# Attention with shared key projections: two batches a matmul, the last key apart, 64-row products in halves of the array

## What is computed

```python
q = (layernorm(x) @ Wq + bq)        # x: 64 x 32 x 256
k = (ctx @ Wk + bk)                 # ctx: 64 x 257 x 192, Wk: 192 x 256
v = (ctx @ Wv + bv)
attn = softmax(clip(q . k * 0.25, -1e4, 1e4))   # per batch, 16 heads of 16
x = x + (attn @ v) @ Wo + bo
```

## Time and profile before

| | before |
|---|---|
| median of 3 runs | 633.14 us (629.55 to 634.79) |
| the profiled execution | 629.26 us, its span 627.5 us |
| granted TensorE clock, mean of the profiled execution | 0.989 |
| busy: PE, PEld, DVE, ACT, POOL | 95%, 77%, 73%, 54%, 53% |
| first stage, start of the first projection to the last scores | 15.6 to 333.1 us |
| the rest up to the end of the span | 333.1 to 627.5 us |

### The profile page before, as it was taken

One profiled execution on the slowest core, in us unless ns is written; L12 is line 12 of the kernel. 1 busy time (PEld: TensorE's weight loads), 2 busy tenths in 40 slices (PEclk: granted clock), 3 DMA queues, 4 the chain that ended last, 5 costly groups with the idle time before them and its releaser, 6 DMA issues. The chain is left out here.

```text
span 627.5 us, 21706 instructions
## 1 busy us (share of the span) xinstructions
PE 596.4 (95%) x8364; PEld 484.3 (77%) x8364; DVE 459.9 (73%) x1073; ACT 339.7 (54%) x743; POOL 331.5 (53%) x482
## 2 busy tenths in 40 slices
PE   9999999999999999999999999896999999998786
PEld 3788878888788887888886788773578888884574
DVE  3687877888678786777776755989799977773453
ACT  3677868788688776778774346541222233330121
POOL 3357858777677885788872322221433333306561
PEclk9999999999999999999999999996999999999999
DMA  8624643766355836973300992119533433435774
GB/s 242 154 68 108 175 167 110 237 180 206 115 172 162 215 127 202 231 209 123 123 3 22 413 412 99 35 49 373 183 127 128 141 136 126 129 116 154 207 210 117
DMA packets 65204, 102.10 MB, mean 163 GB/s; under 512 B 15408, under 2 KB 42096, under 8 KB 64080
## 3 DMA queue, kind: packets, MB, share of 16 engines
q1 hardware_dynamic: 59808, 86.42, 42.7%
q0 software_dynamic: 4432, 13.50, 7.8%
q10 hardware_dynamic: 864, 0.79, 0.5%
HBM read 69.42 MB, written 31.26 MB: 160 GB/s over the span
## 5 line engine op out<-in xcount | busy, mean ns | idle before, releaser
L537 DVE TENSOR_SCALAR Pm<-scores 128x514 f32<-128x514 f32 x128 | 88.1, 688 | 57.0 <-PE scores L750 56.9
L653 ACT ACTIVATE Pm<-Pm,nm 128x257 f32<-128x257 f32 x256 | 115.8, 505 | 2.5 <-DVE nm L542 2.5
L542 DVE TENSOR_REDUCE nm<-Pm 128x2 f32<-128x514 f32 x128 | 87.5, 684 | 2.2
L1634 POOL DMA_INDIRECT Xg<-y_d,inv x39 | 37.1, 951 | 87.1 <-PE scores L1821 69.9
L648 ACT ACTIVATE PT<-bank 128x512 f32<-128x512 f32 x64 | 38.2, 598 | 74.5 <-PE bank L761 74.5
L731 PE MATMUL bank<-hA,wH 128*128 128x258 f32 x256 | 75.3, 305 | 0.1
L738 PE MATMUL bank<-wH,hA 128*128 128x256 f32 x256 | 74.3, 301 | 0.5 <-DVE PT L549 0.5
L761 PE MATMUL bank<-cst,Pm 128*128 128x128 f32 x512 | 69.9, 279 | 0.0
L731 PE MATMUL bank<-hA,wL 128*128 128x258 f32 x256 | 69.1, 280 | 0.0
L738 PE MATMUL bank<-wL,hA 128*128 128x256 f32 x256 | 68.9, 280 | 0.0
L1836 PE MATMUL bank<-W,xh 128*128 x208 | 66.7, 402 | 1.0 <-DVE xl L1744 1.0
(11 more groups left out here) (262 smaller groups left out, 1442.2 us busy)
## 6 DMA issues: line engine op xcount, KB each, us to landing
w_d<-whl SPq DMA_DIRECT2D x64, 256.0 KB, 3.4
W<-w_d SPq DMA_DIRECT2D x8, 2048.0 KB, 15.4
g_d<-gg SPq DMA_DIRECT2D x39, 256.0 KB
wst<-in_W1T SPq DMA_DIRECT2D x32, 256.0 KB, 3.6
cx<-in_ctxT SPq DMA_DIRECT2D x31, 258.0 KB, 2.9
cx<-in_ctxT SPq DMA_DIRECT2D x62, 129.0 KB, 3.5
bb<-in_b SPq DMA_DIRECT2D x8, 512.0 KB, 12.6
xb<-in_x SPq DMA_DIRECT2D x4, 512.0 KB, 5.5
```

What stands on the lines that cost most here:

```text
L537: v.tensor_scalar(Pm[:, i % 2, 2 * p:2 * p + 2, :], S4[:, 2 * p:2 * p + 2, 0:NK], -CLAMP, CLAMP, ALU.max, ALU.min).then_inc(s_cl, 1)
L542: v.tensor_reduce(nm[:, i % 2, 2 * p:2 * p + 2], Pm[:, i % 2, 2 * p:2 * p + 2, :], AX.X, ALU.max, negate=True).then_inc(s_nm, 1)
L653: a.activation(Pm[:, i % 2, g, :], Pm[:, i % 2, g, :], ACT.Exp, bias=nm[:, i % 2, g:g + 1]).then_inc(s_ex, 1)
L1634: g.indirect_dma_start(out=Xg[:, i % 3, :], out_offset=None, in_=y_d, in_offset=bass.IndirectOffsetOnAxis(ap=inv[:, i:i + 1], axis=0)).the ...
```

## The change

**Keys in pairs.** `kproj(j, m)` now projects the 256 first keys of both batches of pair j in one matmul of 512 columns, for one half m of the output channels. A turn of the loop makes one of them (m = i mod 2, pair i // 2 + 1) and the values of batch i+2, where it made both halves of the keys and the values of batch i+1. Both halves of pair 0 are projected ahead of the loop, and the values of batches 0 and 1 in turn 0, after its scores. The last two turns project nothing. `kevac` writes both batches at once, 512 columns.

**The 257th keys.** They are projected once for all 64 batches ahead of the query projection, in the bank of the block `take("x")` (four matmuls of 64 columns, plain float32), and VectorE adds the bias (`kL`). GpSimd copies two columns of them into `kT` every second turn.

**The last 64 channels.** `hA[:, b, 1]` now holds the high parts on all 128 partitions, and `wL[:, 1]` holds the weights' full copy on partitions 0 to 63 and their low part on 64 to 127, so that one matmul of 128 rows gives high x high + high x low. What is left, low x high, is a matmul with 64 rows: on partitions 0 to 63 for the keys (last of the five, 512 columns), on partitions 64 to 127 for the values (first two of the ten, 256 columns). `lA` gets the low parts of these channels. ScalarE makes one more copy for `wL` at the start.

```diff
-        uses = [(("t", 0, k), s_t0e, k + 1) for k in range(2)] + [(("x",), s_vxe, 2)] + [(("q", 0, m), s_qe, m + 1) for m in range(2)]
-        for i in range(-1, T + 1):
+        uses = [(("t", 0, k), s_t0e, k + 1) for k in range(2)] + [(("x",), s_vxe, 4)] + [(("q", 0, m), s_qe, m + 1) for m in range(2)]
+        uses += [(("k", 0, m), s_ke, m + 1) for m in range(2)]
+        for i in range(T + 1):
+            if i == 0:
+                uses += [(("v", b), s_ve, b + 1) for b in range(2)]
             if 1 <= i:
                 uses += [(("p", i - 1, p), s_pte[p], i) for p in range(2)]
-            if i + 1 < T:
-                uses += [(("k", i + 1, p), s_ke, 2 * (i + 1) + p + 1) for p in range(2)]
-            if i + 1 < T:
-                uses += [(("v", i + 1), s_ve, i + 2)]
+            if i + 2 < T:
+                uses += [(("k", i // 2 + 1, i % 2), s_ke, i + 3)]
+                uses += [(("v", i + 2), s_ve, i + 3)]
             if i == 0:
                 uses += [(("b",), s_basee, 1)]
...
-                    i = 2 * j - 5 + n // 4
+                    i = 2 * j - 6 + n // 4
...
-                        sp.wait_ge(s_k, 2 * i + 4)
+                        sp.wait_ge(s_k, i + 3)
                     if n % 4 == 3:
-                        sp.wait_ge(s_v, i + 2)
+                        sp.wait_ge(s_v, i + 3)
...
+                    if i % 2 == 0:
+                        if i == 0:
+                            g.wait_ge(s_vxe, 4)
+                        g.tensor_scalar(kT[:, (i // 2) % 2, :, :, NK - 1], kL[:, :, i:i + 2], 1.0, 1.0, ALU.mult, ALU.mult
+                                        ).then_inc(s_qb, 1)
...
-                    j, n = (i + 3) // 2 if i % 2 else (i + 2) // 2, 0 if i % 2 else 2
+                    j, n = (i + 3) // 2 if i % 2 else (i + 4) // 2, 2 if i % 2 else 0
...
                 v.wait_ge(s_wh, 1)
-                v.tensor_tensor(wL[:, :, :], wA[:, :, :], wH[:, :, :].bitcast(F32), ALU.subtract).then_inc(s_wl, 1)
+                v.tensor_tensor(wL[:, 0, :], wA[:, 0, :], wH[:, 0, :].bitcast(F32), ALU.subtract).then_inc(s_wl, 1)
+                v.tensor_tensor(wL[64:128, 1, :], wA[64:128, 1, :], wH[64:128, 1, :].bitcast(F32), ALU.subtract
+                                ).then_inc(s_wl, 1)
...
+                for m in range(2):
+                    v.tensor_scalar(kL[:, m, :], held("x")[:, C + T * m:C + T * m + T], bcol[:, 2 + m:3 + m], None, ALU.add
+                                    ).then_inc(s_vxe, 1)
...
+                a.activation(wL[0:64, 1, :], wA[0:64, 1, :], ACT.Copy).then_inc(s_wh, 1)
...
-                def kevac(i, m):
-                    a.wait_ge(s_k, 2 * i + m + 1)
-                    if i >= 2:
-                        a.wait_ge(s_s, 2 * (i - 1))
-                    a.activation(kT[:, i % 2, m, :], held("k", i, m)[:, 0:NKP], ACT.Identity, bias=bcol[:, 2 + m:3 + m]
-                                 ).then_inc(s_ke, 1)
+                def kevac(j, m):
+                    a.wait_ge(s_k, 2 * j + m + 1)
+                    if j >= 2:
+                        a.wait_ge(s_s, 4 * (j - 1))
+                    a.activation(kT[:, j % 2, m, :, 0:NB], held("k", j, m)[:, :].rearrange("p (b n) -> p b n", b=2),
+                                 ACT.Identity, bias=bcol[:, 2 + m:3 + m]).then_inc(s_ke, 1)
...
-                        kevac(i + 1, 0)
-                        kevac(i + 1, 1)
-                    if 0 <= i < T:
+                    if i == 0:
+                        vevac(1)
+                    if i + 2 < T:
+                        kevac(i // 2 + 1, i % 2)
+                    if i < T:
                         exps(i, 2)
                         exps(i, 3)
-                    if i + 1 < T:
-                        vevac(i + 1)
+                    if i + 2 < T:
+                        vevac(i + 2)
...
-                def terms(b, bi):
-
-                    hi0, hi1 = hA[:, b, 0, bi, :], hA[:, b, 1, bi, :]
-                    lo0 = lA[:, b, bi, :]
-                    return [(hi0, wH[:, 0, :]), (hi0, wL[:, 0, :]), (lo0, wH[:, 0, :]),
-                            (hi1, wH[:, 1, :]), (hi1, wL[:, 1, :])]
-
-                def kproj(i, m):
-                    b = take("k", i, m)
-                    t.wait_ge(s_lo, 2 * (i // 2 + 1))
-                    for e, (c, w) in enumerate(terms((i // 2) % 2, i % 2)):
-                        mm = t.matmul(b[:, 0:NKP], w[:, 128 * m:128 * m + 128], c, start=(e == 0), stop=(e == 4))
-                    mm.then_inc(s_k, 1)
+                def terms(x, w):
+                    return [(x(hA, 0), w(wH, 0)), (x(hA, 0), w(wL, 0)), (x(lA, 0), w(wH, 0)), (x(hA, 1), w(wL, 1))]
+
+                def kproj(j, m):
+                    b = take("k", j, m)
+                    t.wait_ge(s_lo, 2 * (j + 1))
+                    for e, (c, w) in enumerate(terms(lambda a, n: a[:, j % 2, n, :, :].rearrange("p b n -> p (b n)"),
+                                                     lambda a, n: a[:, n, 128 * m:128 * m + 128])):
+                        t.matmul(b[:, :], w, c, start=(e == 0), stop=False, skip_group_check=True)
+                    t.matmul(b[:, :], wH[0:64, 1, 128 * m:128 * m + 128],
+                             lA[0:64, j % 2, 1, :, :].rearrange("p b n -> p (b n)"), start=False, stop=True,
+                             skip_group_check=True).then_inc(s_k, 1)
 
                 def vproj(i):
                     b = take("v", i)
+                    j = (i // 2) % 2
                     for c in range(2):
-                        for e, (x, w) in enumerate(terms((i // 2) % 2, i % 2)):
-                            mm = t.matmul(b[:, C * c:C * c + C], x[:, 128 * c:128 * c + 128], w[:, C:2 * C],
-                                          start=(e == 0), stop=(e == 4))
+                        t.matmul(b[:, C * c:C * c + C], lA[64:128, j, 1, i % 2, 128 * c:128 * c + 128],
+                                 wH[64:128, 1, C:2 * C], start=True, stop=False, skip_group_check=True)
+                    for c in range(2):
+                        for e, (x, w) in enumerate(terms(lambda a, n: a[:, j, n, i % 2, 128 * c:128 * c + 128],
+                                                         lambda a, n: a[:, n, C:2 * C])):
+                            mm = t.matmul(b[:, C * c:C * c + C], x, w, start=False, stop=(e == 3), skip_group_check=True)
                     mm.then_inc(s_v, 1)
 
                 def scores(i):
-                    t.wait_ge(s_qb, i + 1)
-                    t.wait_ge(s_ke, 2 * i + 2)
+                    t.wait_ge(s_qb, i + 1 + i // 2 + 1)
+                    if i % 2 == 0:
+                        t.wait_ge(s_ke, i + 2)
                     if i:
                         t.wait_ge(s_cl, 2 * i)
                     for g in range(4):
                         r = slice(32 * g, 32 * g + 32)
                         for m in range(2):
-                            mm = t.matmul(B[g][64 * m:64 * m + 64, 0:NKP], QF[r, i % 2, m, :], kT[r, i % 2, m, :],
+                            mm = t.matmul(B[g][64 * m:64 * m + 64, 0:NK], QF[r, i % 2, m, :], kT[r, (i // 2) % 2, m, i % 2, 0:NK],
                                           start=True, stop=True, skip_group_check=True)
                         if g % 2:
...
-                    mm = t.matmul(b[0:T, 0:C], c256[0:K, k, :], wA[0:K, k, C:2 * C], start=(k == 0), stop=(k == 1))
+                    t.matmul(b[0:T, 0:C], c256[0:K, k, :], wA[0:K, k, C:2 * C], start=(k == 0), stop=(k == 1),
+                             skip_group_check=True)
+                for m in range(2):
+                    for k in range(2):
+                        K = 128 - 64 * k
+                        mm = t.matmul(b[:, C + T * m:C + T * m + T], wA[0:K, k, 128 * m:128 * m + 128], c256[0:K, k, :],
+                                      start=(k == 0), stop=(k == 1), skip_group_check=True)
                 mm.then_inc(s_vx, 1)
                 qproj(0)
...
+                t.wait_ge(s_wl, 2)
+                t.wait_ge(s_wh, 2)
+                kproj(0, 0)
+                kproj(0, 1)
+                for i in range(T + 2):
+                    if i < T:
                         scores(i)
+                    if i == 0:
+                        vproj(0)
+                        vproj(1)
...
-                    if i + 1 < T:
-                        for p in range(2):
-                            kproj(i + 1, p)
-                        vproj(i + 1)
+                    if i + 2 < T:
+                        kproj(i // 2 + 1, i % 2)
+                        vproj(i + 2)
```

More of the change, by code:

```diff
@@ L16 @@
 NKP = 258
+NB = 256
 VH = 17
@@ L447, in _ @@
                 spread(0)
[L448 removed]
+                g.wait_ge(s_qb, 2)
                 split(1, 3)
@@ L809, in base_row @@
                     mm.then_inc(s_base, 1)
-                t.wait_ge(s_wl, 1)
-                for i in range(-1, T + 2):
-                    if 0 <= i < T:
+                t.wait_ge(s_wl, 2)
[3 more added lines that the diff above has]
```

(5 more changed lines are left out.)

28 lines of the change are left out of this document (15 added, 13 removed).

## The result

The changed kernel takes 637.09 us (median of 12 runs, 635.71 to 640.01), the kernel before 631.64 (median of 12, 628.80 to 635.35). The ratio is 1.0085, with a 95% interval of 1.0061 to 1.0109: 5.4 us slower. That is under the one per cent by which the prediction divided "same" from "slower", with the interval's upper end over it; the interval also shows that twelve runs of each tell 0.85% from nothing, which is finer than the prediction thought. Forecast were 639 and +6.2 us, in a range of 629 to 652. The case that came is thus "same" by the forecast's own bound (chance 0.37), not the likelier "slower" (0.50). The profiled execution has a span of 634.6 us where before had 627.5.

The account below looks back on a forecast made before the run. TensorE's issue sequence was taken to bound the first stage. Start +5.2, turns +2.0 and end -1.0 summed to +6.2 us on the median of 633.1, giving 639.3, rounded 639, in a range of 629 to 652.

Parts of the forecast that it names:

- The bound: First stage: TensorE, busy 316.3 of 317.5 us, sets the time; what it issues in a turn is what a turn costs.
- The price of changing the array's rows: Steady turn, around the 64-row pair: two partition changes, each 0.1 us of emptying and 0.1 of a load in the open.
- The overlap of the two halves: Steady turn: the values' two 64-row products run hidden beside the keys' 64-row product, giving back 0.24 us.
- The bubble: Last piece of a turn: 0.1 us wait of the values' bank for VectorE's copy L549, expected to go.
- Rival D: First stage does not move: turn 0.05 to 0.1 us shorter, the start eats it, 633 to 636 us; chance 0.15.
- Turns: Steady turn +0.03 us, for the 61 turns from batch 1 to batch 62 that project: +2 us.
- The start: Ahead of batch 1's scores: 257th-key block +1.4, keys of pair 0 +1.3, two value projections +2.5; scores 5.2 us late.
- The end: Last turns: batch 62's no longer projects and VectorE sets the distance to the clip of batch 63; -1.0 us.
- The wide key copy: ScalarE in a turn: two key copies (0.83 us together) become one of 128x512, like L648's 0.60.
- The few late turns: Turns where more is queued on GpSimd may cost 1 us together, left to the range.
- VectorE's turn gates nothing: Steady turn: the whole VectorE turn is under 4.3 us and holds nothing up.
- the doubled width: Keys in a turn: five 512-column matmuls take 1.14 us where ten took 1.20, saving only 0.06.

Follow-up runs that it names:

- e1: Changed kernel with every 64-row product made 128 rows high, low products of the last 64 channels counted twice; 624.57 us beside 627.81 before.
- e5: Changed kernel with the three 64-row matmuls moved directly ahead of the scores in 26 even turns; 629.18 us against 628.61 before, ratio 1.001.
- e2: Changed kernel with the values' 64-row products on partitions 0 to 63, where the keys' one also is; 645.55 us, before 627.81 on this chip.
- e4: Wide keys without 64-row products, plus a wait of the values for VectorE's copy of transposed bank p=1; 631.08 us.
- v1: Changed kernel without its 64-row products: wide keys and 257th keys apart, last 64 channels as before; 624.51 us against 627.81 before, ratio 0.9948.
- v5: Changed kernel without 64-row products, start reordered, ScalarE making the last channels' high parts, 257th keys' start flag corrected; 619.33 us against 628.40 before, ratio 0.9869.
- e3: Changed kernel with the 257th keys' matmuls reordered by row height and batch 0's values projected before its scores; 630.18 us beside 627.70 before.
- e6: Kernel of e5 with the start of e3 and each bank's start flag on its first matmul alone; 626.47 us against 628.40 before, ratio 0.9971.

## Why the prediction held, point by point

**Right, and shown by an experiment.** The bound (TensorE's own sequence, turn by turn; e1 changes nothing but the height of products in it, and the turn follows). The price of changing the array's rows beside products of 256 and 512 columns: I took 0.2 us for each change, from the earlier trace rows; e5 measured 0.20, e1 the sum of both and what they save (+0.17 a turn; mine was 0.4 - 0.24 = +0.16). The overlap of the two halves (e2: without it +0.23 a turn, mine 0.21). The bubble, the short idle time of TensorE, that VectorE's copy made (e4). The steps in the timeline: load at +0.32, full values at +0.43, VectorE's copy no longer gating. Rival D (turns 0.05 to 0.1 shorter, 633 to 636) falls with the turn, which is 0.04 longer; the total of 637.09 alone would hardly have settled it.

**Right in size.** Turns +0.04 where I said +0.03; from batch 1's scores to batch 62's +2.27 us where I said 2.0, of which 0.5 is longer late turns (below). The start, less VectorE's 1.11: 5.45 where I said 5.2, in its parts +1.45 for the block (12.48 to 15.08 = 2.60, before 1.15; I said 1.4), +1.44 to the first scores (from the first key product's work, 18.63, to 22.53 = 3.90, before 2.46; I said 1.3), +2.54 between the scores of batches 0 and 1 (I said 2.5). The end -1.17, I said -1.0. The two score times that I gave, 21.2 and 28.4, came 1.3 later each (22.56, 29.71): 1.1 of it by VectorE's late normalisation. Where that is absent (e2, e5) they are 21.27 and 28.66, and 21.26 and 28.44.

**Off.** The wide key copy was taken as 0.60, by L648, which copies without a bias; it took 0.69. In the start it stands on the path and is most of what lacked in the 1.3. The few late turns I left to the range: 32 and 56 (5.23), where the keys wait for GpSimd's low parts, and four at 4.9, of which 26 and 52 also wait for GpSimd. They cost 1.1 us, where before lost 0.6 in three. That VectorE's turn gates nothing was said of the loop and holds there; for the start I took VectorE's time as that of before, and there one operation ran 1.06 us longer. And the 6.2 us were set on the first median of before, 633.1, which was 1.5 above its later one; the difference, +5.4, is 0.8 below mine, where the ratio's interval leaves 1.5 open to either side. That the forecast of 639 lies only 2 above the measured 637 is therefore part sum and part chance of the medians; the parts are the better test. (The 5,120 and 5,160 columns of the prediction are those of two turns.)

**The weak term.** I wrote that the doubled width saves 0.06 us and the bubble 0.1. v1 gains 0.12 for their sum of 0.16: by the timeline of v5 four wide products take 0.93 (203.81 to 204.74), five thus 1.16 where ten narrow ones took 1.20, so 0.04 is the width and 0.08 the bubble. And I named them as two gains that stand beside each other. e4 shows that the first hangs on the second: without the change of banks the width saves nothing, since the shorter keys only end earlier before the same copy.

**Of the edits, then:** wide keys in pairs and the 257th keys apart gave 0.12 us a turn, the 64-row products took 0.16 a turn back, and the start cost 5.5 (4.1 of it without the 64-row products), of which the end gave 1.2 back. The part whose aim was fewer columns on the array made the kernel slower than before.

## What to carry to other kernels

Cutting rows of a product saves no time of TensorE unless another product runs beside it, and each change of the rows in use has a price (here 0.2 us beside products of 256 and 512 columns, nearly that of a product of 512 columns, and 0.14 among products of twice 64); put such products where the array changes its rows anyway, or leave them at full height. Beside the scores the pair was even slightly cheaper than at full height (turns of 4.62 against 4.65 to 4.67, read across kernels). When a piece of a loop gets shorter, look first whether a wait ends at its end, and in which turns another engine has least slack, since those turns give the gain back. What is moved ahead of a loop to be done once is paid in the open.

## What was not expected of the hardware

- A change of rows costs the same from 128 to 64 as back, and a change of columns alone (64 to 128 at 64 rows, e3) delays the next load as much: 0.30 us behind the last pass ahead of it, in e3 as in the changed kernel, where the rows change at that place too. Beside the keys the next load comes 0.32 us after the 512-column product began to work, where the next product usually works at 0.23, and it works itself 0.11 later. The row shows the wait as `[0.36 <-issue]`, as if nothing were waited for.
- VectorE's normalisation (two inputs of 256 columns by 128 partitions, 0.48 us) waited for an operation of GpSimd that had begun 0.01 us ahead of it, and ended 0.28 us behind it: 1.54 us. It recurs in the loop: in before two such normalisations (at 70.50 and 222.77) took 0.90, each begun 0.7 behind GpSimd's L403 and ended 0.28 behind its end. VectorE's clip at 204.21 of the changed kernel, which reads a bank, took its usual 0.68 with GpSimd's L408 running (203.80 to 205.08). The pattern is read from the rows of all thirteen executions; no run moved GpSimd's operation to test it. At the start all else waits for this operation, so one profiled execution can put over 1 us on a change that didn't cause it.
- Two halves of 64 rows ran in two banks with different widths (512 and twice 256 columns) at full rate, in accumulation too (e5, e6): a start or a running sum makes no difference in time.
